# The last groups' scatters dealt differently to two accumulators, and a new order of the final additions and stores

## The reference

```
xn  = layernorm(x)
out = x + attention(xn) + moe(xn)
attention(xn): linear attention with 16 heads, output projection, residual,
               then gamma * (y - mean) * rsqrt(var + 1e-3) + beta
moe(xn):       shared(xn) + sum over the 8 best of 64 experts of gate * expert(xn)
shared, expert: (xn @ up1) * silu(xn @ up2) @ down       (128 -> 384 -> 128)
```

## Time and profile before

| | us |
|---|---|
| median of three runs | 361.5 |
| their range | 359.62 to 364.17 |
| the profiled execution's own time | 357.78 |
| its span, first to last instruction | 355.9 |
| TensorE busy (matmul) | 329.7 |
| GpSimd busy | 258.1 |
| VectorE busy | 262.6 |
| mean granted TensorE clock | 0.981 of full |

### The profile page before, as it was taken

The page is one execution under the profiler, slowest core; times in us unless marked ns, Lnnn a source line. Parts: engine busy times, 40 slices in busy tenths (PEclk is TensorE's granted clock), DMA queues, the critical chain, the costliest instruction groups (busy, mean ns, idle before and its releaser), DMA issues.

```text
span 355.9 us, 9262 instructions
## 1 busy us (share of the span) xinstructions
PE 329.7 (93%) x3059; PEld 310.6 (87%) x3059; DVE 262.6 (74%) x1070; ACT 206.7 (58%) x450; POOL 258.1 (73%) x259
## 2 busy tenths in 40 slices
PE   8999877699999999999999999999999998999991
PEld 7889776598989998989999998999999998889991
DVE  5898982677767577878787787778777865756566
ACT  4889713537465677565565957473767555574220
POOL 5977765165777887787888777878887787757645
PEclk9999998799999999999999999999999999999998
DMA  7999723289878887878878777878787878753795
GB/s 214 350 379 315 168 59 99 104 231 344 215 173 202 199 197 197 193 190 193 213 172 227 164 211 179 196 186 220 173 203 173 193 176 235 167 130 32 196 356 173
DMA packets 60126, 71.15 MB, mean 200 GB/s; under 512 B 14896, under 2 KB 47920, under 8 KB 60080
## 3 DMA queue, kind: packets, MB, share of 16 engines
q1 hardware_dynamic: 42736, 56.47, 50.8%
q0 software_dynamic: 15360, 13.12, 23.8%
q10 hardware_dynamic: 1984, 0.98, 0.9%
HBM read 54.72 MB, written 15.43 MB: 197 GB/s over the span
## 4 chain that ended last, share of the span: by engine, by line
PE 67%; ACT 10%; DVE 7%; DMA 6%; issue 6%; POOL 2%; another core or an unknown queue 1%; SPq 1%; DVEq 0%; POOLq 0%; ACTq 0%
PE bank L1404 27%; PE bank L1414 11%; PE bank L1323 5%; PE bank L1337 3%; DMA ew<-acc 3%; PE bank L1438 3%; PE bank L1451 3%; PE bank L1423 3%; ACT L584 2%; PE bank L1491 2%; ACT L697 1%; PE bank L1457 1%; PE bank L1370 1%; PE bank L1483 1%; PE bank L1430 1%
## 5 line engine op out<-in xcount | busy, mean ns | idle before, releaser
L539 POOL DMA_INDIRECT acc<-ys,idx_g x64 | 105.4, 1648 | 33.6 <-issue 15.3
L1404 PE MATMUL bank<-xe,ew 128*128 128x160 f32 x768 | 119.4, 305 | 5.6 <-ACT xe L637 4.8
L1404 PEld LDWEIGHTS bank<-xe,ew 128*128 128x128 f32 x768 | 111.1, 194 | 8.8 <-ACT xe L637 5.4
L520 POOL DMA_INDIRECT gath<-xng,idx_g x80 | 81.7, 1021 | 36.2 <-issue 20.7
L612 ACT ACTIVATE si<-bank 128x480 f32<-128x480 f32 (+1 forms) x96 | 52.0, 542 | 66.1 <-PE bank L1323 26.9
L833 DVE TENSOR_TENSOR ac<-si,bank 128x480 f32<-128x480 f32 x64 | 41.7, 651 | 27.6 <-ACT si L612 21.3
L1414 PE MATMUL bank<-ew,ac 128*128 128x128 f32 x384 | 57.2, 284 | 1.4 <-issue 0.9
L1414 PEld LDWEIGHTS bank<-ew,ac 128*128 128x128 f32 x384 | 49.9, 195 | 3.1 <-issue 2.5
L1323 PE MATMUL bank<-xT,shw 128*128 128x128 f32 x384 | 50.0, 278 | 0.0
L1323 PEld LDWEIGHTS bank<-xT,shw 128*128 128x128 f32 x384 | 46.5, 192 | 0.4 <-ACT cum L737 0.2
L654 ACT ACTIVATE ys<-bank,gath 128x128 f32<-128x128 f32 x64 | 23.3, 364 | 18.9 <-PE bank L1414 16.2
(11 more groups left out here) (169 smaller groups left out, 576.4 us busy)
## 6 DMA issues: line engine op xcount, KB each, us to landing
ew<-in_expert_w SPq DMA_DIRECT2D x64, 384.0 KB
ew<-in_expert_w SPq DMA_DIRECT2D x64, 192.0 KB
ew<-acc SPq DMA_DIRECT2D x8, 512.0 KB, 7.2
xng<-xn SPq DMA_DIRECT2D x8, 256.0 KB, 5.2
acc<-zeros SPq DMA_DIRECT2D x4, 512.0 KB, 5.4
acc<-betas SPq DMA_DIRECT2D x4, 512.0 KB
x_sb<-in_x SPq DMA_DIRECT2D x7, 256.0 KB, 6.2
gath<-xng,idx_g POOLq DMA_INDIRECT x80
```

Of the source, the lines that this page charges most:

```text
L520: pool.indirect_dma_start(out=gath[:, p, m, :], out_offset=None, in_=xng, in_offset=bass.IndirectOffsetOnAxis(ap=idx_g[:, g % 5, m:m + 1], ...
L539: pool.indirect_dma_start(out=acc[adds_to[g, m]], out_offset=bass.IndirectOffsetOnAxis(ap=idx, axis=0), in_=src, in_offset=None, compute_o ...
L1404: last = pe.matmul(h_view(n, half_ + 1, CAP)[:, c, :], ew[p][m][:, k * P:(k + 1) * P], xe[:, p, m, :], start=True, stop=True)
```

## The change

Four things are changed, all of them for the end of the program.

1. `adds_to`: the pieces (14, 3) and (14, 4) now go to `acc0`, and all five pieces of group 15 to `acc1`. So `acc0` gets nothing more after (14, 4), and `acc_landed(0)` waits for no piece of group 15. It waits for each accumulator's last eight scatters instead of its last five.
2. POOL's eight final additions are cut to two: `acc1` onto blocks 2 and 3.
3. VectorE gets the others: `acc0` onto all eight blocks (`add_first`) and `acc1` onto blocks 0, 1, 4, 5, 6 and 7 (`add_second`). The `add_first` are spread over tiles 23 to 28.
4. The stores are dealt to SP (blocks 0, 4, 6, 3 and the last tile) and ACT (blocks 1, 2, 5, 7).

```diff
+    adds_to.update({(NG - 2, 3): 0, (NG - 1, 0): 1, (NG - 2, M): 0})
+    adds_to.update({(NG - 1, m): 1 for m in range(1, M + 1)})
+    finals = (0, 1, 4, 5, 6, 7)
...
-                for g, m in [u for u in scatters if adds_to[u] == k][-M - 1:]:
+                for g, m in [u for u in scatters if adds_to[u] == k][-2 * M:]:
                     sp.wait_ge(s_sc[m], 16 * (g + 1))
...
-            for r in range(4):
-                pool.wait_ge(acc_in[0][RB * r // NA], 16)
-                pool.wait_ge(res_done, RB * (r + 1))
-                pool.wait_ge(y_done, down_at['s', RB * r + RB - 1] + 1)
-                pool.tensor_tensor(x_sb[:, tiles(r), :], x_sb[:, tiles(r), :], acc_back(0, r), ALU.add).then_inc(sum_done, 1)
-            for r in range(4, NR):
-                pool.wait_ge(acc_in[0][RB * r // NA], 16)
+            for r in (2, 3):
                 pool.wait_ge(acc_in[1][RB * r // NA], 16)
-                pool.tensor_tensor(acc_back(0, r), acc_back(0, r), acc_back(1, r), ALU.add).then_inc(both_done, 1)
+                pool.wait_ge(first_done, r + 1)
+                pool.tensor_tensor(x_sb[:, tiles(r), :], x_sb[:, tiles(r), :], acc_back(1, r), ALU.add).then_inc(fin_pool, 1)
...
+            def add_first(r, added):
+                dve.wait_ge(acc_in[0][RB * r // NA], 16)
+                dve.wait_ge(res_done, RB * (r + 1))
+                dve.wait_ge(y_done, down_at['s', added] + 1)
+                dve.tensor_tensor(x_sb[:, tiles(r), :], x_sb[:, tiles(r), :], acc_back(0, r), ALU.add).then_inc(first_done, 1)
```

More of the change, by code:

```diff
@@ L390, in _ @@
             acc_landed(0)
-            for h in range(M):
+            for h in (0, 1, 2, 3):
                 acc_load(0, h)
             acc_landed(1)
-            for h in range(M):
+            for h in (0, 1, 2, 3):
                 acc_load(1, h)
-            for k in range(0, NR, 2):
-                sp.wait_ge(fin_done, k + 1)
-                sp.dma_start(out_n[:, tiles(k), :], x_sb[:, tiles(k), :]).then_inc(out_sem, 16)
+            for r in (0, 4, 6):
+                sp.wait_ge(fin_done, finals.index(r) + 1)
+                sp.dma_start(out_n[:, tiles(r), :], x_sb[:, tiles(r), :]).then_inc(out_sem, 16)
+            sp.wait_ge(fin_pool, 2)
+            sp.dma_start(out_n[:, tiles(3), :], x_sb[:, tiles(3), :]).then_inc(out_sem, 16)
             sp.wait_ge(y_done, down_at['s', NT - 1] + 1)
@@ L791, in _ @@
                 silu(('s', s))
-            for k in range(1, NR, 2):
-                n = slice(RB * k, min(RB * k + RB, NT - 1))
-                act.wait_ge(fin_done, k + 1)
-                act.dma_start(out_n[:, n, :], x_sb[:, n, :]).then_inc(out_sem, 16)
+            act.wait_ge(fin_done, finals.index(1) + 1)
+            act.dma_start(out_n[:, tiles(1), :], x_sb[:, tiles(1), :]).then_inc(out_sem, 16)
+            act.wait_ge(fin_pool, 1)
+            act.dma_start(out_n[:, tiles(2), :], x_sb[:, tiles(2), :]).then_inc(out_sem, 16)
+            act.wait_ge(fin_done, finals.index(5) + 1)
+            act.dma_start(out_n[:, tiles(5), :], x_sb[:, tiles(5), :]).then_inc(out_sem, 16)
+            act.wait_ge(fin_done, finals.index(7) + 1)
+            act.wait_ge(y_done, down_at['s', NT - 2] + 1)
+            act.dma_start(out_n[:, NT - RB:NT - 1, :], x_sb[:, NT - RB:NT - 1, :]).then_inc(out_sem, 16)
         @block.vector
@@ L840, in shared_add @@
                     dve.wait_ge(res_done, s + 1)
-                if s == NT - 1:
-                    dve.wait_ge(fin_done, NR)
+                if s >= first_by:
+                    dve.wait_ge(first_done, s // RB + 1)
+                if s >= second_by:
+                    dve.wait_ge(fin_done, finals.index(7) + 1)
                 where = X if s >= NT - LATE and s % 2 == 1 else Y
@@ L1217, in add_second @@
                 dve.tensor_tensor(x_sb[:, tiles(r), :], x_sb[:, tiles(r), :], acc_back(1, r), ALU.add).then_inc(fin_done, 1)
-            def add_both(r):
-                dve.wait_ge(both_done, r - 3)
-                dve.wait_ge(res_done, RB * (r + 1))
-                dve.wait_ge(y_done, down_at['s', min(RB * r + RB, NT - 1) - 1] + 1)
-                dve.tensor_tensor(x_sb[:, tiles(r), :], x_sb[:, tiles(r), :], acc_back(0, r), ALU.add).then_inc(fin_done, 1)
-            finish(NG - 2)
-            for s in range(NT - LATE, 28):
-                shared_mul(s)
-                if s == 24:
-                    finish(NG - 1)
-                shared_add(s)
+            finish(NG - 2)
@@ new lines, in _ @@
+            shared_mul(22)
+            shared_add(22)
+            shared_mul(23)
+            add_first(0, 22)
+            shared_add(23)
+            shared_mul(24)
+            finish(NG - 1)
+            shared_add(24)
+            shared_mul(25)
+            add_first(1, 24)
+            add_first(2, 24)
+            shared_add(25)
+            shared_mul(26)
+            add_first(3, 25)
+            add_first(4, 25)
+            shared_add(26)
+            shared_mul(27)
+            add_first(5, 26)
@@ L1232, in _ @@
+            add_first(6, 26)
+            shared_add(27)
             shared_mul(28)
-            add_second(0)
-            add_second(1)
+            add_first(7, 27)
+            add_second(0, 27)
             shared_add(28)
             shared_mul(29)
-            add_second(2)
-            add_second(3)
+            add_second(1, 28)
             shared_mul(30)
-            add_both(4)
+            add_second(4, 28)
+            shared_mul(31)
             shared_add(29)
-            shared_mul(31)
@@ L1243, in _ @@
-            add_both(5)
             shared_add(30)
-            add_both(6)
-            add_both(7)
+            add_second(5, 30)
+            add_second(6, 30)
+            add_second(7, 30)
             shared_add(31)
```

8 lines of the change are left out of this document (5 added, 3 removed).

## The result

The changed kernel takes **367.21 us** (median of four runs, 363.27 to 370.71), the kernel before in the same comparison 360.56 us (four runs, 356.71 to 364.17). The ratio is 1.0198, with a 95% interval of 1.0127 to 1.0269: slower, by about 7 us; whether by more than 2% the interval leaves open. A ratio in this document compares only the faster executions of two kernels, those within 1.5% of their kernel's fastest, so it isn't the quotient of the medians, which are over all runs. The forecast was 366.9 us, and +5.4 us.

The account below looks back on a forecast made before the run. TensorE was taken as the bound, busy 93% of the span, with scatters, loads and POOL's addition setting the end. Stall 5.3, clock 2.0, additions 0.3 and end -2.2 made +5.4 on 361.5: 366.9 us, range 361.5 to 370.5.

Parts of the forecast that it names:

- The chain of causes: Near the end: late scatters delay POOL's pow, finish(15) and down projection 25; stall +5.3 us, low clock +2.0.
- the row of scatters: POOL, group 15: each piece waits for the previous landing; 4.2, 5.3 and 3.7 us, (15, 4) issued at about 337.3.
- the stall: VectorE at finish(15) waits for the late pow: 5.3 us, 2.6 to 6.4 by the bounds.
- the upper bound: For (15, 2) beside acc0's loads: 5.81 us, the price of the dearest scatter, (14, 1), while expert weights came in.
- The sentence that I set beside the sum: DMA queues: by the packet rule (15, 2) would rather take 5.8 us, and the scatters' sum be 0.5 us higher.
- pace and clock together: After the stall, up to shared_add(28): low TensorE clock +2.0 us, VectorE's additions +0.3.
- VectorE's additions and their pace: Between finish(15) and shared_add(28): 8.8 us of VectorE work where 8.1 were available, put at +0.3 us.
- the disturbance: Behind shared_add(28): POOL's two additions slow VectorE by 0.7 us, within the end's 7.2 us, -2.2 in all.
- Lighter: Rival: at finish(15) a 2.6 to 3.5 us stall without the clock's cost; +0.7 to +3.4 us, chance 0.20.
- Heavier: Rival: scatters 5.81 us each beside loads, stall 6.4 or more, clock low for 6.4; +7.7, 369.2 us; chance 0.20.
- Not slower: Rival: pow not late for VectorE at finish(15), late loads decide the end; -1.9 us, 359.6; chance 0.10.
- The change doesn't free `acc0`: Rival: acc0's loads still late, add_first waits behind the same pow at no cost; 366.9 us, no separate chance.

Follow-up runs that it names:

- pow_early: The changed kernel with the last sequence's pow put ahead of the scatter of (15, 1); 363.10 us, 1.0177 of the kernel before.
- deal_pow: The kernel before with only the new dealing of scatters, and the pow ahead of (15, 1); 360.04 us, 1.0124 of the kernel before.
- deal_only: The kernel before with only the new dealing of scatters, POOL's eight additions and the old orders kept; 366.65 us, 1.0332 of the kernel before.
- pow_late: The kernel before with only the pow made late, POOL waiting for acc0's second load ahead of it; 367.92 us, 1.0249 of the kernel before.
- finals_only: The changed kernel with the old dealing of scatters, keeping the new orders of additions and stores; 358.04 us, 1.0117 of the kernel before.
- seconds_last: The changed kernel with the pow ahead of (15, 1) and VectorE's acc1 additions behind shared_add(30); 362.98 us, 1.0016 of the kernel before.
- held: The changed kernel with the pow ahead of (15, 1) and acc0's loads held until the last scatter landed; 365.15 us, one run.
- the two filled kernels: Unread matmuls of ones in TensorE's idle time: 28 in the changed kernel (1.0306), 34 in the kernel before with the pow made late (1.0204).
- filled: The changed kernel with 28 unread matmuls of ones on TensorE between up projection 26 and down projection 25; 367.53 us, 1.0306 of the kernel before.

## Why the prediction was right, and where it was lucky

**The chain of causes** was as forecast: the row of scatters, the `pow` behind it, `finish(15)` behind that, `shared_mul(25)` and down projection 25 behind that, then the clock. pow_early and deal_pow take the stall away, deal_only and pow_late make it without the additions, and finals_only, 1.2% over before, leaves VectorE's additions no more than a part. In the times it is shown by deal_only against deal_pow and by seconds_last against the changed kernel; pow_early alone doesn't show it there, because its second wait, for `acc1`, took the place of the first.

**The step that was mis-sized** is the row of scatters. "4.2 us for (15, 1) ... 5.3 for (15, 2) ... and 3.7 for (15, 3)" was 3.88, 8.54 and 3.56 in the profile. The middle one, beside the loads, was 3.2 us longer than I took and 2.7 above the upper bound, which was the dearest scatter beside the weights' loads. The sentence that I set beside the sum went the right way: the Trainium skill ("DMA: Bandwidth & Descriptors", section "Queues, rings and completion order") has each DMA engine change queues only after whole packets. By its rule I had moved only to 5.8, and no run here shows whether that rule is the reason. The kernels that ran loads beside scatters had the three intervals at 13.4 to 16.0 us in all, held at 10.7. So the stall was 8.2 us in this profile instead of 5.3, and 7.1 to 8.6 in the other kernels that left the `pow` behind the scatters.

**The other terms** can be read between fixed points. From `finish(15)`'s beginning to `shared_add(28)` it was 9.38 us before and 12.02 after: +2.6, where pace and clock together were put at +2.3. The low clock reached 5.7 us into the work, more than the 3.3 us and less than the 6.4 I took it from, and cost 0.8 to 1.9 us by the two filled kernels, which leaves 0.7 to 1.8 us for VectorE's additions and their pace, where I had put 0.3. From `shared_add(28)` to the last addition's end it was 9.35 and 6.76: -2.6, where -2.2 was forecast. One addition beside POOL's took about 1.2 us instead of 0.68 (a pair 1.84, at 347.56), within its bounds, but ahead of `shared_add(28)`, where I had put the disturbance behind it. Behind the last addition it is 3.3 us instead of 2.8, where three stores of blocks had been issued less than 1.1 us before that of the last tile (two before the change): +0.45 that I had put at nothing. That these stores are the reason was not tested. Together: 8.2 + 2.6 - 2.6 + 0.5 = +8.7, of the +8.8 of the stretch.

**So the sum was +5.4 where the stretch shows +8.8 and the medians +6.65.** That the time of 366.9 us came within 0.3 us of the median of 367.21 is luck. I had added 5.4 us to a median of 361.5, and in the comparison the kernel before had 360.56: its 0.9 us less and the effect's 1.25 us more nearly cancel. The runs spread over 7.4 us besides, and why the medians differ by less than the stretches stays open. That (15, 2)'s delay varies from one execution to the next is likely, given 6.4 us in filled, which has the same loads and scatters, but I have no trace of the same kernel twice.

**The rivals.** "Lighter" falls: the wait was 8.2 us and the clock fell. Its price was too wide too, since 3.5 us without the clock make 3.5 + 0.3 - 2.2 = +1.6, not +3.4. "Heavier" named the right direction: its stall of 6.4 us or more came true, though not by 5.81 us for every scatter but by 8.5 for one. Its clock term did not: the low clock reached 5.7 us, not 6.4, and by the filled kernels it cost 0.8 to 1.9 us, not 3.2. "Not slower" had its price worked out from the late loads; pow_early and seconds_last show that with no stall these do come to decide, as it said, though at 30.5 to 31.5 us and not at the 25.9 that -1.9 us would mean. It had priced the landing of (15, 4) with the 5.3 us of the forecast, and had not seen that TensorE would be held up behind `add_second(0)`. "The change doesn't free `acc0`" falls: its loads were issued at 322.55, 1.5 us after (15, 1), where about 2 were forecast.

## What to carry to other kernels

Before dealing work to queues anew, look at what stands behind the last item in the same engine's program: here a `pow` of 1.3 us, which had been ready 1.6 us before it was needed, carried 6 to 7 us of deal_only's loss (deal_only against deal_pow), and moving it delayed (15, 1) by only 0.65 us (2.51 us after (14, 4) in pow_early, 1.86 in the changed kernel). A buffer that is free earlier doesn't help if the other one, whose items now stand in one row, comes later by more: 10.7 us for three scatters in a row against 6.3 before, even with nothing beside them. And a bulk load sent off in the middle of short DMAs that wait for each other must be priced by what it adds to each of them.
